# Narrow attention: values behind the scores, product in the spare bank ahead of the second turn

## What is computed

```
q = (x @ Wq + bq).reshape(B, Tx, 16, 16).transpose(0, 2, 1, 3)
k = (xf @ Wk + bk).reshape(B, Txf, 16, 16).transpose(0, 2, 1, 3)
v = (xf @ Wv + bv).reshape(B, Txf, 16, 16).transpose(0, 2, 1, 3)
scores = jnp.einsum('bhqd,bhkd->bhqk', q * 0.25, k)
probs = jax.nn.softmax(scores, axis=-1)
attn = jnp.einsum('bhqk,bhkd->bhqd', probs, v)
out = attn.transpose(0, 2, 1, 3).reshape(B, Tx, 256) @ Wo + bo
```

## Time and profile before

| What | Value |
|---|---|
| median of 3 runs | 1667.96 us (1666.09 to 1669.24) |
| time of the profiled execution | 1667.43 us |
| its span | 1665.6 us |
| PE busy | 1496.8 us (90%) |
| PE weight loads | 1225.9 us (74%) |
| DVE busy | 976.1 us (59%) |
| ACT busy | 909.0 us (55%) |
| POOL busy | 409.8 us (25%) |
| mean granted TensorE clock | 0.969 |

### The profile page before, as it was taken

The page is one execution under the profiler, slowest core; times in us unless marked ns, Lnnn a source line. Parts: engine busy times, 40 slices in busy tenths (PEclk is TensorE's granted clock), DMA queues, the critical chain, the costliest instruction groups (busy, mean ns, idle before and its releaser), DMA issues. The chain is left out here.

```text
span 1665.6 us, 36296 instructions
## 1 busy us (share of the span) xinstructions
PE 1496.8 (90%) x12206; PEld 1225.9 (74%) x12206; DVE 976.1 (59%) x2020; ACT 909.0 (55%) x2528; POOL 409.8 (25%) x679
## 2 busy tenths in 40 slices
PE   5999999699999999999999979986888888788787
PEld 4787787588877887888788768875667666666576
DVE  5547365756776776667666654446646556464443
ACT  3547364546655655666465543334656566565454
POOL 2011010341203121211211100005635555463100
PEclk9999999899999999999999979997999999999799
DMA  8000000020000000000000010001000000000000
GB/s 236 2 1 0 0 0 0 26 84 8 13 7 7 7 7 7 7 7 7 7 7 7 7 62 16 0 0 31 16 16 9 15 16 16 8 15 8 1 23 22
DMA packets 26176, 30.22 MB, mean 18 GB/s; under 512 B 1459, under 2 KB 24056, under 8 KB 25848
## 3 DMA queue, kind: packets, MB, share of 16 engines
q1 hardware_dynamic: 26104, 29.20, 6.0%
HBM read 27.36 MB, written 1.84 MB: 18 GB/s over the span
## 5 line engine op out<-in xcount | busy, mean ns | idle before, releaser
L795 ACT ACTIVATE B_probs<-banks,B_neg_max 112x375 f32<-112x375 f32 x256 | 145.0, 571 | 155.7 <-DVE B_neg_max L876 155.7
L1574 DVE TENSOR_REDUCE D_neg_max<-banks 112x2 f32<-112x750 f32 x128 | 114.2, 934 | 120.5 <-PE banks L1690 120.5
L876 DVE TENSOR_REDUCE B_neg_max<-banks 112x1 f32<-112x375 f32 x256 | 128.1, 542 | 93.9 <-PE banks L966 93.6
L1477 ACT ACTIVATE D_probs<-banks,D_neg_max 112x375 f32<-112x375 f32 x256 | 143.7, 574 | 40.2 <-DVE D_neg_max L1574 40.2
L769 POOL TENSOR_TENSOR B_q_hi<-B_q_group,ones 128x112 fp32r<-128x112 f32 x128 | 48.5, 379 | 341.6 <-PE banks L966 314.2
L632 PE MATMUL banks<-B_ctxT,B_wk_hi 128*128 128x378 f32 x390 | 123.1, 370 | 1.5 <-DVE B_wq_lo L865 1.5
L1697 PE MATMUL banks<-ident,D_probs 112*126 112x112 f32 x780 | 98.1, 262 | 13.1 <-ACT D_ctx_full L1497 7.7
L992 PE MATMUL banks<-B_probsT,B_v 126*64 126x112 f32 x1584 | 105.9, 269 | 0.0
L884 DVE TENSOR_SCALAR B_probs<-B_probs,B_rsums 112x375 f32<-112x375 f32 x258 | 100.7, 432 | 4.6
L976 PEld LDWEIGHTS banks<-ident,B_probs 112*126 112x126 f32 x786 | 86.8, 140 | 18.2 <-DVE B_probs L884 1.9
L337 ACT ACTIVATE A_probs<-banks,A_neg_max 112x112 f32<-112x112 f32 x256 | 87.0, 367 | 21.9 <-DVE A_neg_max L411 20.8
(11 more groups left out here) (323 smaller groups left out, 3976.6 us busy)
## 6 DMA issues: line engine op xcount, KB each, us to landing
ctx<-in_ctx_dram SPq DMA_DIRECT2D x35, 189.0 KB
ctx<-in_ctx_dram SPq DMA_DIRECT2D x35, 92.2 KB
w_stage<-in_L_xattn_Wq_dram SPq DMA_DIRECT2D x2, 1024.0 KB, 8.2
w_stage<-in_L_xattn_Wp_dram SPq DMA_DIRECT2D x1, 2048.0 KB, 8.0
w_stage<-in_L_xattn_W_dram SPq DMA_DIRECT2D x2, 1024.0 KB, 6.5
out_dram<-x_tokens SPq DMA_DIRECT2D x4, 448.0 KB, 3.2
x_tokens<-in_x_dram SPq DMA_DIRECT2D x1, 1344.0 KB, 20.3
w_stage<-in_L_xattn_Wk_dram SPq DMA_DIRECT2D x1, 1024.0 KB, 9.9
```

The source lines that it names most:

```text
L795: nc.scalar.activation(P[:, u % PS, j, 0:S], SB[j][0:N, 0:S], ACT.Exp, bias=nm[:, u % PS, j:j + 1], accum_out=sm[:, u % PS, j:j + 1]).then ...
L876: nc.vector.tensor_reduce(nm[:, u % PS, j:j + 1], SB[j][0:N, 0:S], AX.X, ALU.max, negate=True).then_inc(max_done, 1)
L1477: nc.scalar.activation(P[:, m % 2, j, 0:S], SB[0:N, j, 0:S], ACT.Exp, bias=nm[:, m % 2, j:j + 1], accum_out=sm[:, odd, 4 * m + j:4 * m + j ...
L1574: nc.vector.tensor_reduce(nm[:, m % 2, 2 * half:2 * half + 2], SB[0:N, 2 * half:2 * half + 2, 0:S], AX.X, ALU.max, negate=True).then_inc(m ...
```

## The change

In narrow attention alone:

- The buffer of turned probabilities PT (D_probsT) gets a second half by the step's parity; both copies write the half (m - 1) % 2.
- PE's order in a step becomes scores, values, product, second turn, then (fourth batch) the query product, then the first turn. The values are those of head group m - 2 instead of m - 1. The wait for pt_act moves ahead of the values, the wait for pt_dve from ahead of the values to ahead of the first turn and of what stands before it.
- In a fourth batch DVE copies the keys (semaphore k_dve) and ACT all four query products (q_act); before it was keys by ACT and queries by both. The helper keys_out picks the semaphore. DVE's copy of the second turn moves behind its other work there.
- POOL: the context split goes ahead of the query split and its wait; the scaling of the raw values moves from the second to the third step, as ACT's copy of the raw values moves behind the second step's exponentials.
- Behind the loop one more product of values.

```
-        PT = sb("probsT", [ST, 4, NS * N])
+        PT = sb("probsT", [ST, 2, 4, NS * N])
...
+        def keys_out(eng, g, b, n):
+            if b < 3:
+                eng.wait_ge(k_act, 6 * g + 2 * b + n + 1)
+            else:
+                eng.wait_ge(k_dve, 2 * g + n)
```

In the program of POOL, in a step:

```
-                        if m == 1:
-                            keys_split(2 * t + 1, 1)
-                        if m == 3:
-                            keys_split(2 * t + 2, 0)
+                        if m == 0:
+                            context_split(t + 1, 1 - b % 2)
+                        if m % 2:
+                            keys_out(pool, g, b, 1 + m // 2)
+                            keys_split(2 * t + 1 + m // 2, 1 - m // 2)
+                        if m == 2:
+                            o_scaled(t)
                         pool.wait_ge(s_done, 4 * t + m + 1)
                         if b == 3:
-                            pool.wait_ge((q_dve, q_act)[m % 2], 2 * g + 3 + m // 2)
+                            pool.wait_ge(q_act, MT * g + m + 3)
                         queries_split(g, t + 1, (b + 1) % GB, m)
-                        if m == 0:
-                            context_split(t + 1, 1 - b % 2)
-                        if m == 1:
-                            o_scaled(t)
```

In the program of ACT, in a step:

```
-                        pt_evac(i)
+                        pt_evac(i, (m - 1) % 2)
...
-                        if m % 2 == 0 and b == 3:
-                            keys(2 * t + 1 + m // 2, 1 - m // 2)
...
-                        if m % 2 and b == 3:
+                        if m == 1:
+                            raw_values(t)
+                        if b == 3:
                             act.wait_ge(ql_done, 4 * t + m + 1)
                             queries(g * MT + MT + m + 1, m, PJ)
```

In the program of DVE, in a step:

```
                         maxima(i, m, 0)
                         maxima(i, m, 1)
-                        pt_evac(i)
-                        if m == 0:
+                        if b != 3:
+                            pt_evac(i, (m - 1) % 2)
+                        if m % 2 == 0 and b == 3:
+                            keys(2 * t + 1 + m // 2, 1 - m // 2)
+                        if m == 0 and b != 3:
                             rsums_out(t)
...
-                        if m % 2 == 0 and b == 3:
-                            dve.wait_ge(ql_done, 4 * t + m + 1)
-                            queries(g * MT + MT + m + 1, m, PJ)
+                        if b == 3:
+                            pt_evac(i, (m - 1) % 2)
+                        if m == 0 and b == 3:
+                            rsums_out(t)
```

In the program of PE, in a step:

```
                         scores(t, m)
...
                         if m == 2:
                             pe.wait_ge(raw_out, t + 1)
                             pe.wait_ge(v_out, 2 * (t + 1))
-                        values(1 - odd if m == 0 else odd, (m - 1) % 4)
+                        pe.wait_ge(pt_act, i + 1)
+                        values(odd if m >= 2 else 1 - odd, (m - 2) % 4, m % 2)
                         if b == 3:
+                            product(g, b, t, m, odd)
+                            second_turn(g, b, t, m)
...
                             queries(m, PJ)
+                        else:
+                            product(g, b, t, m, odd)
+                            second_turn(g, b, t, m)
                         pe.wait_ge(exp_done, 16 * t + 4 * m + 2 + EXP0)
+                        pe.wait_ge(pt_dve, i + 1)
                         if m == 0:
                             pe.wait_ge(rb_dve, t + 1)
                             rsums(1)
-                            turn(0, 0)
...
-                            turn(m, 0)
+                        turn(m, 0)
```

More of the change, by code:

```diff
@@ L1575, in maxima, with pt_evac, keys @@
                                         ALU.max, negate=True).then_inc(max_done, 1)
-            def pt_evac(i):
+            def pt_evac(i, par):
                 dve.wait_ge(t_done, 2 * i + 2)
-                nc.vector.tensor_copy(PT[:, 2:4, :], TB[0:ST, :, 0:NS * N]).then_inc(pt_dve, 1)
+                nc.vector.tensor_copy(PT[:, par, 2:4, :], TB[0:ST, :, 0:NS * N]).then_inc(pt_dve, 1)
+            def keys(n, c):
+                dve.wait_ge(k_mm, n + 1)
+                dve.wait_ge(k_lo, n)
+                nc.vector.tensor_scalar(kf[:, :], PJ[:, 0:SP], bk[:, c:c + 1], None, ALU.add).then_inc(k_dve, 1)
             def two_values(n, odd, bank):
@@ L1712, in tokens_turn, with values @@
                                         ).then_inc(ln.turned, 1)
-            def values(odd, m):
+            def values(odd, m, par):
                 for s in range(NS):
@@ L1719, in values @@
                                                v[:, odd, s, h, :, :].rearrange("p r d -> p (r d)"),
-                                               PT[:, j, s * N:(s + 1) * N], start=(s == 0), stop=(s == NS - 1),
+                                               PT[:, par, j, s * N:(s + 1) * N], start=(s == 0), stop=(s == NS - 1),
                                                tile_position=(0, 32 * j))
@@ L1738, in _ @@
                 queries(m, SB[:, m, :])
-            pe.wait_ge(k_out, 1)
+            pe.wait_ge(k_act, 1)
             new_values(0, 2, PJ[0:ST, 0:D])
@@ L1752, in _, with product, second_turn @@
             pe.wait_ge(v_out, 2)
+            def product(g, b, t, m, odd):
+                if b == 3 and m:
+                    pe.wait_ge(q_act, MT * g + m + 2)
+                if m == 0:
+                    pe.wait_ge(y_out, t + Y0)
+                    if b == 0:
+                        pe.wait_ge(q_act, MT * g + 2)
+                    keys(odd, 1)
+                if m == 1:
+                    keys_out(pe, g, b, 1)
+                    pe.wait_ge(c_lo, 2 * (t + 2))
+                    new_values(1 - odd, 0, PJ[0:ST, 0:D])
+                    new_values(1 - odd, 1, PJ[0:ST, D:2 * D])
+                if m == 2:
+                    pe.wait_ge(v_out, 2 * (t + 1) + 1)
+                    keys(1 - odd, 0)
+                if m == 3:
+                    keys_out(pe, g, b, 2)
+                    new_values(1 - odd, 2, PJ[0:ST, 0:D])
+                    pe.wait_ge(o_out, t + 1)
+                    project()
+            def second_turn(g, b, t, m):
+                pe.wait_ge(pt_act, 4 * t + m + 1)
+                if m == 0:
+                    pe.wait_ge(c_out, NS * (t + 1))
+                    pe.wait_ge(rce_done, t + 1)
+                    rsums(0)
+                if m == 1:
+                    pe.wait_ge(rb_act, t + 1)
+                if m > 1:
+                    pe.wait_ge(c_out, NS * (t + 1) + m - 1)
+                if b == 0 and m == 3:
+                    tokens_turn(g + 1, 0)
+                if b == 1 and m:
+                    tokens_turn(g + 1, m)
+                turn((m - 1) % 4, 1)
             with pe.Fori(0, NG) as g:
@@ L1798, in _ @@
-                        pe.wait_ge(pt_dve, i + 1)
-                        if m == 1:
+                        if m == 2:
                             pe.wait_ge(raw_out, t + 1)
                             pe.wait_ge(v_out, 2 * (t + 1))
-                        values(1 - odd if m == 0 else odd, (m - 1) % 4)
+                        pe.wait_ge(pt_act, i + 1)
+                        values(odd if m >= 2 else 1 - odd, (m - 2) % 4, m % 2)
                         if b == 3:
+                            product(g, b, t, m, odd)
+                            second_turn(g, b, t, m)
@@ L1824, in _ @@
                             context_turn(m - 1, TB[:, 0, SPARE:SPARE + ST], TB[:, 1, SPARE:SPARE + ST])
-                            turn(m, 0)
+                        turn(m, 0)
             pe.wait_ge(pt_act, 4 * B + 1)
+            values(1, 2, 0)
             pe.wait_ge(c_out, NS * (B + 1))
@@ L1832, in _ @@
             pe.wait_ge(pt_dve, 4 * B + 1)
-            values(1, 3)
             pe.wait_ge(rb_dve, B + 1)
             rsums(1)
+            values(1, 3, 1)
             pe.wait_ge(o_out, B + 1)
```

61 lines of the change are left out of this document (11 added, 50 removed).

## The result

The changed kernel takes 1686.32 us (median of 4 runs, 1685.32 to 1689.79), the kernel before beside it 1667.70 (4 runs, 1666.09 to 1669.24). The ratio is 1.0115, 95% interval 1.0098 to 1.0133: slower by 1.15%. The direction of the forecast held and the range did by 0.7 us: its upper end was 1687, and one of the four runs lies above it. The size did not hold. Forecast were +5.5 us; the medians differ by 18.6 and the profiled executions by 17.9 (1685.32 against 1667.43; spans 1683.5 against 1665.6).

A forecast was written before the change was run, and what follows sets the result against it. PE's sequence with its waits was taken to bound the kernel. Ordinary steps +28.8, fourth batches -22.0, lower clock there -2.3 and behind the loop +1.0 made +5.5 us, median 1673.5 us, range 1660 to 1687.

The forecast's parts named there:

- PE's order in ordinary steps: First three batches of each group: VectorE's copy of the second turn is late once in every step, +28.8 us.
- my pieces: Start-to-start times from the earlier trace, added to ordinary steps of 5.67, 5.54, 5.20 and 6.60 us.
- The tokens' +0.55: Steps turning the next group's tokens, one in first and three in second batches: transposes and another VectorE copy, +0.55 us each.
- The old cover: Ordinary steps before the change: VectorE's maxima and copy run beside turn and product, which hides 0.85 us of copy.
- The fourth batch: Fourth batches: earlier context split ends PE's wait, steps one to three shorten, -22.0 us; lower clock behind it goes, -2.3 us.
- Rival 3: Fourth batches: GpSimd is late all the same, long wait and low clock stay, +19 us, 1693; chance 0.05.
- rival 2: PE's gaps: the clock falls in them; 1.15 us in every first step makes +18 us, 1692; chance 0.10.
- a granted clock of 0.50 inside ordinary steps: Ordinary steps: one of the listed signs that the forecast is wrong.
- The loop's jump: Fourth batch's step four and the jump behind it, PE standing 1.82 us: no change, 0.
- Ahead and behind the loop: Behind the loop: one more product of values, +0.7, and a longer wait for the sums, +0.3; +1.0 us.
- Rival 1: Values, product and second turn without waits: joined groups issue faster, 11.5 us saved, 1662.0; chance 0.15.
- My own case: Whole kernel: +5.5 us, median 1673.5, spanning 1668 to 1679 for 0.08 us error in each of 64 steps; chance 0.70.

The follow-up runs named there:

- runs 3: Changed kernel with the values moved, in a group's first three batches, from behind the scores to behind the second turn: 1641.45 us, ratio 0.9823.
- 4: Changed kernel with VectorE's copy of the second turn cut to one of its two banks: 1661.96 us, ratio 0.9971.
- Run 6: Kernel before the change, with VectorE's copy of the second turn cut to one of its two banks: 1652.45 us, ratio 0.9913.
- Run 1: Kernel before the change, with only GpSimd's context split moved ahead of the query split and its wait: 1650.75 us, ratio 0.9885.
- Run 7: Changed kernel run once more, unedited, for a second trace: 1684.74 us, ratio 1.0121.
- run 2: Changed kernel with GpSimd's context split put back behind the query split and its wait: 1700.91 us, ratio 1.0175.

## Why the prediction was right and where it was wrong

**PE's order in ordinary steps: the mechanism right, the sum 4.4 us short.** That the copy is late in every step is what the timeline shows, and runs 3 and 4 tie it to the copy: cover it and a step falls by 0.9 us (0.65 of it the wait), halve it and a step falls by 0.35. Forecast +28.8, measured +33.2 at full clock. The four steps are 0.06, 0.17, 0.10 and 0.07 over my pieces. In the third step: scores to values 0.98 where I had 0.90 (PE goes on 0.14 us behind ScalarE's copy, not 0.06), turn to context turn 1.74 where I had 1.69, the rest within 0.03. In the second step turn to context turn is 1.87. The failing piece is the release of an engine: I took the shortest one, 0.05 us, from the earlier trace rows, and the new waits take 0.10 to 0.23. The text named 0.08 a step as 5 us; that is about what happened. The tokens' +0.55 was right in sum (+0.63, +0.48, +0.66, +0.48).

**The old cover.** I wrote that VectorE's chain beside turn and product is what hides the copy, and that nothing now hides it. Run 6 shows that half the copy was worth its whole 0.35 us before, in eight ordinary steps of twelve, so it was hidden in four of twelve only; what changed in the others is when the copy starts. The sum did not suffer, since it was made from starts and not from that statement.

**The fourth batch: right.** Forecast -22.0 and -2.3, measured -24.3. GpSimd starts its split 1.94 us into the first step (forecast about 2), takes 3.54 (3.5) and ends 1.85 us before it is needed (1.8). The second step is 6.05 (6.07), first and third 5.73 and 5.74 (5.7 both). Rival 3 is out, and in these three steps so is ScalarE's load as a cost. Run 1 adds what I did not separate: three quarters of this is GpSimd's move and needs none of PE's.

**The clock: the term that failed most.** My sum gave the lower clock nothing after the change, leaving it to rival 2 with a chance of 0.10. In the profiled execution three groups begin, behind the stage's start or the loop's jump, with a step of 6.73 or 7.11 us (5.55 at full clock) and one of their second steps has 7.25: 5.85 us, less 0.63 that the kernel before had in one first step, +5.2. Run 7 has five such steps, four of them at other places. The row of windows behind the jump shows 0.50. I had named a granted clock of 0.50 inside ordinary steps as a sign of being wrong; it came in one second step here (0.51 from 1462 to 1465 us) and in three ordinary steps of run 7. I had argued that the earlier trace rows showed a gap of 1.82 us without harm. That was read at one jump of three. At another of the same trace, behind a gap of 1.73 us, the clock fell (windows, kernel before), and this is where the 0.63 us are:

```profile
1250.00:1252.00 2.00, 2.00 (x10) 2.00 (x9) 2.00 (x4) 1.58 (x6) 2.00 (x4) 0.50 0.00 0
```

The gap at the jump is longer now:

```profile
1350.36 0.74 PE L1710 MATMUL banks<-ident,D_probs 112*126 112x112 f32 x6
...
1351.50 0.42 POOL L1384 TENSOR_TENSOR D_q_lo<-D_q_group,D_q_hi 128x112 fp32r<-128x112 f32 x1
...
1353.48 0.43 PE L1703 MATMUL banks<-D_k_hi,D_q_hi 32*112 32x378 f32 x4 [2.38 <-issue]
```

(timeline of PE and GpSimd, kernel after.) But its length does not decide it: behind this gap of 2.38 us the step took 5.55, at full clock, and behind gaps of 2.34 and 2.73 it took 7.11; in run 7 it was 7.11 behind 2.37, and 5.56 behind 2.76 and 2.43. Rival 2 put the loss at every first step, 18 us; it came at four or five steps of 64, 0.8 to 1.6 us each, 6 to 7 us. The rule cited from the Trainium skill (TensorE: Matmul & The Clock Gate, A second HAM failure mode: psum-queue depth-cycling) tells of a clock that goes up and down with short gaps between groups of matmuls. It is half borne out: the clock does fall behind such gaps, but only in one of the 48 ordinary steps (in run 7 in three), though each of them has a gap of 1.0 to 1.45 us.

**The loop's jump: forecast 0, measured +1.9.** PE stands 2.34 to 2.73 us there, marked "issue", where it stood 1.68 to 1.82. No run here was about the jump. The trace shows where the time is not: at the jump shown above GpSimd's last query split ends 1.56 us after PE's last turn has started, and at this one of the kernel before 1.63 after it. From that end to PE's next scores it is 0.79 us here and 1.56 there (0.79 to 0.92 at the three jumps before, 1.52 to 1.90 now):

```profile
1440.36 0.74 PE L1697 MATMUL banks<-ident,D_probs 112*126 112x112 f32 x6
...
1441.57 0.42 POOL L1378 TENSOR_TENSOR D_q_lo<-D_q_group,D_q_hi 128x112 fp32r<-128x112 f32 x1
...
1442.78 0.43 PE L1690 MATMUL banks<-D_k_hi,D_q_hi 32*112 32x378 f32 x4 [1.68 <-POOL D_q_lo L1378]
```

So the queries are not late; what is longer is PE's own way over the jump. The long form also comes with GpSimd's old order (run 2: 9.75, 10.15 and 10.21), and in a smaller measure without any of PE's new one (run 1: 9.85, 9.40, 9.60; run 6, old in both: 9.42, 9.58, 9.22). Why it is longer stays open.

**Ahead and behind the loop:** forecast +1.0, measured +1.9, 0.6 of it ahead of the stage and so no effect of the change.

**Rival 1, joined groups issue faster: out.** Values to product 0.72 and product to turn 0.96 in the new order, against 0.72 and 0.95 as sums of the old pieces. The joins save nothing here.

The sum again: 5.5 forecast + 4.4 (releases) + 5.2 (clock) + 1.9 (jump) + 0.9 (ends) = 17.9. My own case spanned 1668 to 1679, and the time fell above it: the misses all lay on the slow side, and the case's span had a term for one of them only. That the time still lies in the range is luck: its upper end was put at 1687 for the sake of rivals 2 and 3, of which one did not come and the other came to a third.

One thing wasn't tried: VectorE copying tokens or sums ahead of the probabilities, or the turn of the context ahead of the wait for the copy. The turns share the banks TB, and the order of one engine's reads beside another's writes there would have to be arranged anew.

## What to carry to other kernels

When a wait is moved along an engine's program, ask which independent work lies between the producer of the awaited data and the wait: here 0.72 us of values ahead of the product or behind the turn made 1686 or 1641 us out of the same instructions. Test whether a wait that looks covered is: halving the copy gained in the old order too. Split a change that touches two engines into its halves before judging it: GpSimd's half alone gave 18 us, PE's half in the ordinary steps took 33. And when pieces are added from a trace, take the release of a wait from the middle of its rows (0.05 to 0.23 us here), and read the clock behind every instance of a gap: the jump that I read was harmless, and another one in the same trace was not.

## What the runs showed of the hardware

- The clock's fall is not fixed to a place. Two executions of one program had it at different steps (6.73, 7.11, 7.11, 7.25 against 6.37, 7.23, 7.11, 7.23, 8.69), at the start of the stage and behind waits of 1.3 to 2.7 us; other steps passed the same waits at full clock, and at the jump a gap of 1.73 us was followed by the lower level and one of 2.76 was not.
- VectorE's copy out of the banks took 0.86 us for 672 columns and 0.51 for 336: halving saves 0.35, so some 0.16 us of it do not scale. By this line 224 columns would take 0.39; VectorE's copies of tokens and sums take 0.38.
- From the end of a copy to PE's next matmul it took 0.05 us in the earlier trace rows, and 0.10 and 0.23 in two neighbouring steps of the changed kernel.
